# A 128-column transpose in place of a 16-column one, in an attention and butterfly-FFN layer

## What is computed

```
q, k, v = x·w_q, x·w_k, x·w_v                     (per head: 128 -> 64)
probs   = softmax(q·k / 8 + causal mask)
x1      = layernorm(x + (probs·v)·w_o)
h       = gelu(butterfly_up(x1·W_exp + b_exp) + up_bias)   (128 -> 512, 9 butterfly stages)
out     = layernorm(x1 + butterfly_down(h)·W_con + b_con + down_bias)
```

## Time and profile before

| | before |
|---|---|
| median of 3 runs (lowest, highest) | 1101.54 us (1101.34, 1102.37) |
| the profiled execution | 1099.16 us |
| its span, first to last instruction | 1097.10 us |
| TensorE matmul busy | 1057.8 us, 96% of the span |
| VectorE, ScalarE, GpSimd busy | 725.7, 619.2, 754.8 us |
| mean granted TensorE clock | 0.987 |

### The profile page before, as it was taken

How to read it: one execution, slowest core, us unless ns; L and a number is a source line. 1 busy time by engine, 2 the same in 40 slices (tenths; PEclk the granted TensorE clock), 3 DMA queues, 4 the chain that set the end, 5 groups by cost and what they waited for, 6 DMA issues and landing times.

```text
span 1097.1 us, 17976 instructions
## 1 busy us (share of the span) xinstructions
PE 1057.8 (96%) x5816; PEld 710.8 (65%) x5816; DVE 725.7 (66%) x2029; ACT 619.2 (56%) x1246; POOL 754.8 (69%) x722
## 2 busy tenths in 40 slices
PE   4899999999999999999999999999999999998897
PEld 3566666666776666666766666666766666655566
DVE  6667767677657777676667777776667767641655
ACT  3366666666456666666456666666356666653331
POOL 6278878778457788787468777887467887776112
PEclk8799999999999999999999999999999999999999
DMA  7123222232122322222122222222122222201002
GB/s 217 39 69 78 52 70 53 73 78 60 41 68 59 79 78 52 71 51 73 39 79 54 74 59 79 78 52 69 28 59 78 79 58 69 59 21 30 1 19 59
DMA packets 59626, 68.72 MB, mean 63 GB/s; under 512 B 24807, under 2 KB 31243, under 8 KB 59534
## 3 DMA queue, kind: packets, MB, share of 16 engines
q1 hardware_dynamic: 59534, 67.58, 23.8%
HBM read 31.11 MB, written 2.36 MB: 31 GB/s over the span
## 4 chain that ended last, share of the span: by engine, by line
PE 93%; DVE 3%; POOL 1%; DMA 1%; issue 1%; ACT 1%; SPq 1%; POOLq 0%; DVEq 0%; ACTq 0%
PE O L671 24%; PE SC L646 14%; PE WORK L605 13%; PE SC L650 12%; PE WORK L621 6%; PE WORK L634 5%; PE WORK L581 3%; PE WORK L583 3%; PE WORK L733 3%; PE WORK L582 3%; PE SC L724 1%; PE WORK L591 1%; PE WORK L592 1%; PE WORK L724 1%; PE WORK L593 1%; DVE WORK L951 1%
## 5 line engine op out<-in xcount | busy, mean ns | idle before, releaser
L827 ACT ACTIVATE PR<-SC 128x512 f32<-128x512 f32 (+3 forms) x768 | 352.9, 490 | 313.9 <-PE SC L650 233.8
L484 POOL TENSOR_TENSOR SUM<-SUM,PR 128x1024 f32<-128x1024 f32 (+3 forms) x256 | 417.8, 1632 | 11.5
L646 PE MATMUL SC<-QH,KHL 128*128 128x512 f32 (+3 forms) x768 | 271.2, 359 | 3.5 <-ACT PR L827 1.9
L951 DVE CUSTOM_DVE_ANT_0 WORK<-WORK,CMASK 128x128 f32<-128x128 f32 (+3 forms) x512 | 238.7, 519 | 36.1 <-PE WORK L605 34.4
L650 PE MATMUL SC<-QL,KH 128*128 128x512 f32 (+3 forms) x768 | 261.7, 346 | 0.0
L605 PE MATMUL WORK<-KHL,QH 128*128 128x512 f32 (+3 forms) x768 | 225.2, 361 | 4.5 <-DMA KH<-KHL 2.7
L469 POOL TENSOR_SCALAR_AFFINE_SELECT PR<-PR 128x256 f32<-128x256 f32 x256 | 105.4, 412 | 160.4 <-ACT PR L827 159.9
L671 PE MATMUL O<-PR,VLO 128*64 128x512 f32 (+3 forms) x1024 | 207.0, 525 | 0.0
L646 PEld LDWEIGHTS SC<-QH,KHL 128*128 128x128 f32 x768 | 145.2, 189 | 80.3 <-ACT PR L827 46.7
L492 POOL TENSOR_TENSOR SUM<-PR 128x768 f32<-128x768 f32 x64 | 134.8, 2106 | 86.3 <-DVE OT L995 60.7
L605 PEld LDWEIGHTS WORK<-KHL,QH 128*128 128x128 f32 x768 | 132.6, 190 | 71.8 <-issue 52.8
(11 more groups left out here) (102 smaller groups left out, 1097.8 us busy)
## 6 DMA issues: line engine op xcount, KB each, us to landing
QH<-QH SPq DMA_DIRECT2D x128, 128.0 KB, 2.3
KH<-KHL SPq DMA_DIRECT2D x128, 128.0 KB, 2.3
R<-RROW SPq DMA_DIRECT2D x128, 128.0 KB, 2.8
SW<-in_L_ffn_up_weights_dram SPq DMA_DIRECT2D x9, 512.0 KB, 4.7
SW<-_L_ffn_down_weights_dram SPq DMA_DIRECT2D x9, 512.0 KB, 4.6
out_dram<-X SPq DMA_DIRECT2D x8, 256.0 KB, 2.3
QL<-NROW SPq DMA_DIRECT2D x64, 4.0 KB
RCOL<-R SPq DMA_DIRECT2D x64, 4.0 KB
```

Source lines behind the costliest of these rows:

```text
L484: nc.gpsimd.tensor_tensor(total, total, prob(unit, s), ALU.add).then_inc(add_done, 1)
L646: nc.tensor.matmul(dst, KHL[:, par, h, kt * P:(kt + 1) * P], QH[:, par, h, q0:q0 + n], start=True, stop=False)
L827: nc.scalar.activation(prob(unit, s)[:, h, :], SC[use % NSC][:, 0:n], ACT.Exp, scale=K ** -0.5).then_inc(exp_done, 1)
L951: op = nc.vector.tensor_tensor_reduce(cols, cols, CMASK[:, CH - n:], 1.0, LOWEST, ALU.add, ALU.max, cell)
```

## The change

NEGM gets 128 columns. VectorE clears it once at the start, the reduction of line 958 (959 after) still writes its first 16 columns, and the transpose loads all 128 columns and writes 128 partitions of the WORK buffer, of which the first 16 are read as before.

```diff
-        NEGM = sb("NEGM", [P, 2 * TILES])
+        NEGM = sb("NEGM", [P, P])
...
                 elif f[0] == "mt":
                     pe.wait_ge(negm_made, u + 2)
-                    t = nc.tensor.transpose(w[0:2 * TILES, 0:P], NEGM[:, :], IDN[:])
+                    t = nc.tensor.transpose(w[:, 0:P], NEGM[:, :], IDN[:])
...
             nc.vector.memset(QL[0:K, :, 1, :].bitcast(F32), 0.0)
+            nc.vector.memset(NEGM[:], 0.0)
             nc.vector.memset(MP[:], LOWEST).then_inc(rows_set, 1)
...
-                        nc.vector.tensor_reduce(NEGM[:, :], MP[:, :, :], AX_X, ALU.max,
+                        nc.vector.tensor_reduce(NEGM[:, 0:2 * TILES], MP[:, :, :], AX_X, ALU.max,
                                                 negate=True).then_inc(negm_made, 1)
```

## The result

The changed kernel takes 1103.76 us (median of 22 runs, 1102.32 to 1105.89) against 1101.74 us for the kernel before, run beside it 22 times. The ratio is 1.0023, with a 95% interval of 1.0017 to 1.0029: slower by 2.5 us, between 1.9 and 3.2. The two medians themselves are 2.0 us apart, the means 2.6. Forecast were 1103.0 us, in a range of 1101.3 to 1104.9, and 0.13% slower, which is 1.45 us. The time lies in the range, but above the 1102.5 to 1103.4 given to the forecast's own case; the increase was undersized, and it lies on the edge of the 0.2% that was to part "same" from "slower".

A forecast was written before the change was run, and what follows sets the result against it. TensorE's stream was taken to bound the kernel: 31 unit transposes at 0.045 us make 1.40 us, with the start-up 1.45, added to the 1101.54 us median for 1103.0 us, 0.13% slower. The range was 1101.3 to 1104.9 us.

The forecast's parts named there:

- the forecast's own case: Whole kernel: the 128-column transpose load is partly uncovered, giving 1103.0 us, between 1102.5 and 1103.4; chance 0.60.
- TensorE's stream sets the time, and no later wait takes the delay in: Attention units: matmuls fill all 28.50 us of one unit, so the kernel's end gets any added TensorE time in full.
- What counts is the uncovered part of the transpose's own load, and the load behind it stays hidden: Line 610, behind line 671: its load stands uncovered, while line 646's load hides under the streaming identity; 45 ns a unit.
- 45 ns a unit: Line 610: price of loading 112 more columns, taken between 35 and 52 ns; over 31 units 1.40 us.
- the difference of the recorded load durations (52 ns): Line 610: recorded load of 139 ns for 128 transpose columns against 87 for 16; surplus 52 ns as price.
- the scaling of the half-clock row to full clock by the ratio of ordinary loads (35 ns): Line 555's half-clock transpose load, 56 ns against 139 ordinary, gives 0.40; times 102 ns is 41, less 6: 35 ns.
- The start-up transpose: The one transpose in the start-up, at half clock behind waiting for NEGM: its load pays 0.05 us more, once.
- The ordinary price as a rival (96 ns): Line 610: a transpose's load costs what an ordinary one does, 96 ns, 3.1 us in all, 1104.6 us; chance 0.20.
- Clearing NEGM costs nothing: Start-up: clearing takes at most 0.36 us on VectorE, inside 1.65 us of its idle time; counted as nothing.
- the prediction's own sign of being wrong: Whole kernel: the prediction is wrong if time changes at other places, the start-up or the granted clock; no size given.
- Late maxima as a rival: Line 650 of the next unit waits for late maxima; 0.1 us late gives 1106.1; chance 0.05, with other new waits.
- Nothing to be seen, or faster: Line 610: load stays covered, 1101.6 us, chance 0.12; or the 16-column load forced a costly shape change, 1100.9, chance 0.03.

The follow-up runs named there:

- NEGM alone: Kernel before with NEGM widened to 128 columns and cleared, its transpose still loading 16 columns; ratio to the kernel before 1.0003, and 1.0013 when run again.
- the 16-column extras: Kernel before, NEGM untouched, plus 63 transposes of 16 identity columns straight behind line 671 and ahead of the scores; ratio to the kernel before 1.0005.

## Why the prediction was right, and where it was off

- *TensorE's stream sets the time, and no later wait takes the delay in.* Right for the load: the unit after is filled by it as before, and the chain around the transpose grew only in the entry of line 610. In two units out of 31 there was another wait, below.
- *What counts is the uncovered part of the transpose's own load, and the load behind it stays hidden.* Right, and shown from three sides: moved behind a full-width matmul the 128 columns add 1 ns to the record, a second transpose pays no load, and line 646 behind it takes its 0.12 us in all.
- *45 ns a unit.* Undersized: 53. Of the two ways to get at it, the difference of the recorded load durations (52 ns) was right, and the scaling of the half-clock row to full clock by the ratio of ordinary loads (35 ns) was wrong. The forecast took a value between them. 31 × 0.008 = 0.25 us was lost here. The start-up transpose, for which 0.05 us was taken, is recorded with 446 ns at half clock in the second profile of the changed kernel against 373 before, 0.07 us; in the first profile it fell into a stretch at full clock (303 ns), which is no effect of the load.
- *The ordinary price as a rival (96 ns).* Fell: 53 ns in place, and 3.5 us instead of 6.0 in 63 extra transposes. By the Trainium skill, "TensorE: Matmul & The Clock Gate", section "LDWEIGHTS (loading the stationary operand)" (columns divided by 1.2 ns), it would have been, as an estimate from that page, 93 ns for the 112 columns more. The runs show 0.47 ns a column for a transpose's load, so the rule held here for the ordinary load alone, and the measurement decides.
- *Clearing NEGM costs nothing.* Right by the trace of the start-up, where the next operation is not later. But the sum had no term for anything else that comes with the larger, cleared NEGM, and took it for nothing without saying so. The two runs with NEGM alone give 0.3 and 1.4 us, and the three profiles of the changed kernel 0.8 to 1.0 us in two stretches. That is the larger part of what the sum missed, and it is the prediction's own sign of being wrong, that the time changes at other places. That 1103.0 came so near to 1103.76 is in part luck: a term of this size was not foreseen in either direction. It isn't a steady cost of each unit: the median distance between the transposes of neighbouring units is 28.60 and 28.63 us in the two profiles with NEGM alone, and 28.61 and 28.63 in the two of the kernel before.
- *Late maxima as a rival.* Its reason, that the wider transpose delays them, fell: the room at the usual unit is as it was. But the wait itself exists. It is there in the 21st stretch of all nine profiles with the larger NEGM, with 16 columns loaded too, for 0.1 to 0.4 us; it is 0.4 us in the second profile of the kernel before, at another unit; and it is more frequent once the transpose is moved back.
- *Nothing to be seen, or faster.* Fell with the recorded 330 ns; and the account of 0.01 us a unit that today's transpose costs the stream was confirmed by the 16-column extras (0.5 us for 63).

## What to carry to other kernels

A weight load costs what is not covered by the matmul ahead of it. Here it was covered behind full-width matmuls (271 ns recorded) and not behind the 64-column products (330 ns); that the change of width is the reason is likely, but no run here parts it from other traits of those products. Look at such places first, and put the narrowest operand there. A small matmul there is nearly free, since it only takes over the wait that the next full-width load would have had; the same small matmul amid full-width work costs its full streaming time. A buffer that grows, or one more instruction, can also delay a transfer somewhere else: by 0.8 us at the same place in each profile here. It shows when the same stretch is compared in several profiles of either kernel. And for a change of a few tenths of a per cent, take start-to-start times that repeat within one profile rather than the difference of two spans, which here was 6.4 us for a change of 2.5.

## What was not expected of the hardware

A transpose's load of 128 columns costs 53 ns more than one of 16 where nothing covers it, 0.47 ns a column. Beside a covered one it is 59 ns (330 for 271), 0.58 of the ordinary load's 102; at half clock, behind idle time, the ratio had looked smaller (56 to 139, 0.40). Two executions of the same kernel had spans of 1097.1 and 1099.5 us, with waits for small transfers in one and not in the other, and the granted clock was at half for one more stretch of 3.4 us, in the last part, in some executions of either kernel. One small transfer of the sixth stretch landed after 2.2 to 2.4 us in every profile with the larger NEGM and after 1.4 in every one without.
